# The four order tables of a recurrent stage, written anew

## The reference

```
h = layernorm(x) * (1 + ca) + sa;  x = x + ga * attn(h)
h = layernorm(x) * (1 + cb) + sb;  x = x + gb * moe(h)
# attn, per sequence and head (32 pairs), over 4 chunks of 64 tokens, one after the other:
gate = k @ w0;  hb = k @ w2;  hidden = silu(gate) * hb;  dhidden = v @ w1.T
G1 = (hidden * lr1).T @ v;  G0 = (k * lr0).T @ dgate;  G2 = (k * lr2).T @ dhb
wi = wi + newtonschulz(Gi, 2 steps)      # X = a X + (b A + c A A) X, with A = X X.T
wi = wi / norm(wi) * norm(wi at the start)
o  = (silu(q @ w0) * (q @ w2)) @ w1
# then: norm of o, projection, residual; routing logits; experts (64, top 6); combine
```

## Time and profile before

| | |
|---|---|
| median of 3 runs | 1771.67 us |
| the profiled execution | 1769.68 us, its span 1767.3 us |
| PE, DVE, ACT, POOL busy | 90%, 65%, 50%, 46% of the span |
| instructions | 40874 |
| recurrent stage | about 150 to 930 us of the span |

### The profile page before, as it was taken

How to read it: one execution, slowest core, us unless ns; L and a number is a source line. 1 busy time by engine, 2 the same in 40 slices (tenths; PEclk the granted TensorE clock), 3 DMA queues, 4 the chain that set the end, 5 groups by cost and what they waited for, 6 DMA issues and landing times. The chain is left out here.

```text
span 1767.3 us, 40874 instructions
## 1 busy us (share of the span) xinstructions
PE 1591.9 (90%) x11235; PEld 1184.7 (67%) x11235; DVE 1147.2 (65%) x4093; ACT 880.9 (50%) x2156; POOL 817.9 (46%) x882
## 2 busy tenths in 40 slices
PE   7995999888889888988862999999999999998997
PEld 4664667666666666666652677777777777776775
DVE  5664878788888788888864554444444444433887
ACT  4773767666666666666641333333333333332221
POOL 2322334566566566666675233333333343343333
PEclk9996999999999999999965999999999999999998
DMA  3864444444444532232224656556555656322996
GB/s 131 258 226 153 129 143 128 156 134 141 152 150 153 163 95 83 83 89 83 74 89 135 183 175 186 172 171 185 171 175 176 182 179 194 98 54 62 252 245 152
DMA packets 260031, 263.27 MB, mean 149 GB/s; under 512 B 83563, under 2 KB 231385, under 8 KB 259824
## 3 DMA queue, kind: packets, MB, share of 16 engines
q1 hardware_dynamic: 196016, 170.45, 33.4%
q0 software_dynamic: 21504, 51.18, 8.2%
q10 hardware_dynamic: 42304, 39.08, 8.1%
HBM read 141.78 MB, written 127.18 MB: 152 GB/s over the span
## 5 line engine op out<-in xcount | busy, mean ns | idle before, releaser
L1709 POOL DMA_INDIRECT scratch_y<-e_eo,e_goes x256 | 251.7, 983 | 405.3 <-ACT e_eo L1798 336.6
L1735 PE MATMUL e_psGU<-wgu,e_xT 128*128 x1024 | 352.1, 466 | 3.1 <-issue 2.3
L1846 DVE COPY e_hT<-e_psH 88x256 f32<-88x256 f32 x256 | 107.7, 421 | 338.6 <-PE e_psH L1744 242.2
L1751 PE MATMUL e_psD<-wd,e_hT 88*128 x1024 | 263.6, 379 | 0.0
L1735 PEld LDWEIGHTS e_psGU<-wgu,e_xT 128*128 128x128 f32 x1024 | 186.7, 190 | 87.6 <-issue 18.3
L1369 POOL TENSOR_TENSOR f_wnr<-f_wss,f_half 128x4 f32<-128x4 f32 x96 | 109.3, 1139 | 230.7 <-DVE f_wss L1192 230.1
L1359 POOL DMA_INDIRECT scratch_buf<-rows,dest x180 | 185.3, 1030 | 45.5 <-issue 43.7
L1787 ACT ACTIVATE e_sgm<-e_psGU 128x176 f32<-128x176 f32 x256 | 81.2, 317 | 238.5 <-PE e_psGU L1735 206.6
L1751 PEld LDWEIGHTS e_psD<-wd,e_hT 88*128 88x128 f32 x1024 | 173.8, 190 | 14.3 <-issue 0.3
L1798 ACT ACTIVATE e_eo<-e_psD 128x256 f32<-128x256 f32 x256 | 98.1, 383 | 161.8 <-issue 87.6
L1721 PEld LDWEIGHTS e_psX<-ident,e_xg 128*128 128x128 f32 x512 | 72.4, 142 | 76.7 <-issue 40.8
(11 more groups left out here) (303 smaller groups left out, 3773.2 us busy)
## 6 DMA issues: line engine op xcount, KB each, us to landing
e_xg<-scratch_buf ACTq DMA_DIRECT2D x256, 132.0 KB
scratch_y<-f_blank SPq DMA_DIRECT2D x64, 384.0 KB
c_g<-scratch_y SPq DMA_DIRECT2D x64, 384.0 KB, 6.1
...
```

The lines of the kernel that those rows point to most:

```text
L1709: pool.indirect_dma_start(out=T["y"], out_offset=bass.IndirectOffsetOnAxis(goes[:, n:n + 1], 0), in_=eo[:, n % OB, :], in_offset=None, bou ...
L1735: mm = pe.matmul(psGU[:, j % 2, 0:2 * F], xT[:, j % 2, k, :], wgu[:, bass.ds(buf, 1), k, :].rearrange("p b n -> p (b n)"), start=(k == 0), ...
L1751: mm = pe.matmul(psD[:, j % 2, 0:D], hT[0:FH, j % 2, k, :], wd[0:FH, buf, k, :].rearrange("p b n -> p (b n)"), start=(k == 0), stop=(k == 1))
L1846: v.tensor_copy(hT[0:FH, b, :, :].rearrange("p k t -> p (k t)"), psH[0:FH, b, 0:2 * P]).then_inc(htd, 1)
```

## The change

The four tables are replaced. The steps, their waits and the number of times each is issued stay as they are, but for a last "send" entry that issues nothing. The tables start at another point of the cycle (PE's now with the poly2's of lot 1 in the half headed by chain 1), and lags are raised by one where that needs it. Within the cycle entries change places, and the two halves, alike before but for the names of the chains, now differ. Cut to the parts of which the prediction speaks:

PE_ORDER, the half headed by chain 0 before (the other is its mirror), and both halves after:

```diff
-    ("x2t", 1, 1, 2), ("gram2", 1, 1, 1), ("x2", 1, 1, 2, 0), ("output", 1, 2, 1), ("poly2", 1, 1, 0),
-    ("gram2", 1, 1, 2), ("turn_o", 0, 2, 1), ("hidden_back", 0, 0), ("poly2", 1, 1, 1), ("poly2", 1, 1, 2),
-    ("last", 1, 1, 0), ("grads_0", 0, 0), ("project", 0, 2, 0), ("back", 0, 1, 2, 1), ("grads_1", 0, 0),
-    ("last", 1, 1, 1), ("grads_2", 0, 0), ("turn", 0, 0, 0, 1), ("grads_3", 0, 0), ("turn", 0, 0, 1, 0),
-    ("last", 1, 1, 2), ("gram", 0, 0, 0), ("turn", 0, 0, 2, 1), ("row_sums", 0, 0), ("gram", 0, 0, 1),
-    ("turn_x", 1, 3, 1), ("totals", 0, 0), ("read", 0, 1, 0), ("back", 1, 1, 0), ("gram", 0, 0, 2), ("back", 1, 1, 1),
-    ("gate", 1, 0), ("logits", 1, 3, 1), ("poly", 0, 0, 0), ("poly", 0, 0, 1), ("poly", 0, 0, 2), ("x2", 0, 0, 0, 1),
...
+    ("poly2", 0, 1, 1), ("poly2", 0, 1, 2), ("project", 1, 3, 0), ("back", 1, 2, 2, 1), ("grads_0", 1, 1),
+    ("grads_1", 1, 1), ("grads_2", 1, 1), ("last", 0, 1, 1), ("grads_3", 1, 1), ("turn", 1, 1, 0, 1),
+    ("row_sums", 1, 1), ("turn", 1, 1, 1, 0), ("gram", 1, 1, 0), ("last", 0, 1, 2), ("turn", 1, 1, 2, 1),
+    ("gram", 1, 1, 1), ("totals", 1, 1), ("back", 0, 1, 0), ("turn_x", 0, 3, 1), ("read", 1, 2, 0),
+    ("logits", 0, 3, 1), ("back", 0, 1, 1), ("gate", 0, 0), ("gram", 1, 1, 2), ("poly", 1, 1, 0), ("poly", 1, 1, 1),
+    ("poly", 1, 1, 2), ("x2", 1, 1, 0, 1), ("x2t", 1, 1, 0), ("x2t", 1, 1, 1), ("hidden_base", 0, 0),
+    ("x2", 1, 1, 1, 1), ("x2t", 1, 1, 2), ("gram2", 1, 1, 0), ("gram2", 1, 1, 1), ("x2", 1, 1, 2, 0),
+    ("output", 1, 2, 1), ("poly2", 1, 1, 0), ("gram2", 1, 1, 2), ("hidden_back", 0, 0), ("turn_o", 0, 2, 1),
+    ("poly2", 1, 1, 1), ("poly2", 1, 1, 2), ("last", 1, 1, 0), ("last", 1, 1, 1), ("grads_0", 0, 0),
+    ("grads_1", 0, 0), ("back", 0, 1, 2, 1), ("project", 0, 2, 0), ("grads_2", 0, 0), ("turn", 0, 0, 0, 1),
+    ("grads_3", 0, 0), ("turn", 0, 0, 1, 0), ("gram", 0, 0, 0), ("turn", 0, 0, 2, 1), ("row_sums", 0, 0),
+    ("last", 1, 1, 2), ("gram", 0, 0, 1), ("totals", 0, 0), ("turn_x", 1, 3, 1), ("back", 1, 1, 0), ("read", 0, 1, 0),
+    ("logits", 1, 3, 1), ("back", 1, 1, 1), ("gate", 1, 0), ("gram", 0, 0, 2), ("poly", 0, 0, 0), ("poly", 0, 0, 1),
+    ("poly", 0, 0, 2), ("x2", 0, 0, 0, 1), ("x2t", 0, 0, 0), ("x2t", 0, 0, 1), ("hidden_base", 1, 0),
+    ("x2", 0, 0, 1, 1), ("gram2", 0, 0, 0), ("x2t", 0, 0, 2), ("gram2", 0, 0, 1), ("x2", 0, 0, 2, 0),
+    ("output", 0, 1, 1), ("poly2", 0, 0, 0), ("turn_o", 1, 2, 1), ("hidden_back", 1, 0), ("gram2", 0, 0, 2),
+    ("last", 0, 0, 0),
```

ACT_ORDER:

```diff
-    ("xt", 1, 1, 2, 1), ("square", 0, 1, 2), ("h_keep", 0, 3, 1), ("read", 1, 2, 0), ("w", 0, 1, 0), ("w", 0, 1, 1),
-    ("l_keep", 0, 3, 1), ("gate", 0, 0), ("x2", 1, 1, 0, 1), ("o_scale", 0, 2), ("x2t", 1, 1, 0), ("x2t", 1, 1, 1),
-    ("x2", 1, 1, 1, 1), ("a2", 1, 1, 0), ("x2t", 1, 1, 2), ("a2", 1, 1, 1), ("output", 1, 2, 1), ("a2", 1, 1, 2),
-    ("o_square", 1, 2), ("b2", 1, 1, 0), ("o_keep", 0, 2, 1), ("b2", 1, 1, 1), ("x2", 1, 1, 2, 0), ("b2", 1, 1, 2),
-    ("square", 1, 1, 0), ("w", 0, 1, 2, 1), ("x", 0, 0, 0), ("x", 0, 0, 1), ("xt", 0, 0, 0, 1), ("x", 0, 0, 2),
...
+    ("xt", 1, 1, 2, 1), ("h_keep", 0, 3, 1), ("w", 0, 1, 0), ("w", 0, 1, 1), ("gate", 0, 0), ("l_keep", 0, 3, 1),
+    ("o_scale", 0, 2), ("read", 1, 2, 0), ("square", 0, 1, 2), ("x2", 1, 1, 0, 1), ("x2t", 1, 1, 0), ("x2t", 1, 1, 1),
+    ("x2", 1, 1, 1, 1), ("a2", 1, 1, 0), ("x2t", 1, 1, 2), ("output", 1, 2, 1), ("x2", 1, 1, 2, 0), ("a2", 1, 1, 1),
+    ("a2", 1, 1, 2), ("b2", 1, 1, 0), ("b2", 1, 1, 1), ("b2", 1, 1, 2), ("o_square", 1, 2), ("o_keep", 0, 2, 1),
+    ("square", 1, 1, 0), ("x", 0, 0, 0), ("w", 0, 1, 2, 1), ("square", 1, 1, 1), ("x", 0, 0, 1), ("xt", 0, 0, 0, 1),
...
+    ("read", 0, 1, 0), ("w", 1, 1, 1), ("l_keep", 1, 3, 1), ("o_scale", 1, 2), ("gate", 1, 0), ("x2", 0, 0, 0, 1),
+    ("x2t", 0, 0, 0), ("x2t", 0, 0, 1), ("x2", 0, 0, 1, 1), ("a2", 0, 0, 0), ("a2", 0, 0, 1), ("output", 0, 1, 1),
+    ("x2t", 0, 0, 2), ("b2", 0, 0, 0), ("o_keep", 1, 2, 1), ("a2", 0, 0, 2), ("x2", 0, 0, 2, 0), ("b2", 0, 0, 1),
+    ("o_square", 0, 1), ("square", 0, 0, 0), ("w", 1, 1, 2, 1), ("b2", 0, 0, 2), ("x", 1, 0, 0), ("x", 1, 0, 1),
+    ("x", 1, 0, 2), ("square", 0, 0, 1), ("xt", 1, 0, 0, 1), ("xt", 1, 0, 1, 0),
```

DVE_ORDER:

```diff
-    ("totals", 0, 0), ("update", 1, 1, 2), ("pick", 0, 3), ("factors", 1, 1, 1), ("renorm", 1, 1, 1),
-    ("norm_x", 0, 2), ("norms", 0, 0), ("a", 0, 0, 0), ("a", 0, 0, 1), ("a", 0, 0, 2), ("b", 0, 0, 0),
-    ("b", 0, 0, 1), ("row_norms", 1, 1, 2), ("b", 0, 0, 2), ("read", 0, 1, 0), ("place", 0, 3), ("factors", 1, 1, 2),
-    ("gate", 1, 0), ("slope", 1, 0), ("slope_2", 1, 0), ("both", 1, 0), ("token_dg", 1, 0), ("rows_x", 0, 2),
-    ("token_dhb", 1, 0), ("update", 0, 0, 0), ("token_hid", 1, 0), ("row_norms", 0, 0, 0),
...
+    ("token_hid", 0, 0), ("update", 1, 1, 1), ("row_norms", 1, 1, 0), ("squares", 0, 0, 0), ("gate_x", 0, 2, 0),
+    ("row_norms", 1, 1, 1), ("norm_x", 0, 2), ("squares", 0, 0, 1), ("squares", 0, 0, 2), ("factors", 1, 1, 0),
+    ("row_sums", 0, 0), ("renorm", 1, 1, 0), ("totals", 0, 0), ("update", 1, 1, 2), ("factors", 1, 1, 1),
+    ("pick", 0, 3), ("renorm", 1, 1, 1), ("norms", 0, 0), ("a", 0, 0, 0), ("a", 0, 0, 1), ("a", 0, 0, 2),
+    ("b", 0, 0, 0), ("b", 0, 0, 1), ("row_norms", 1, 1, 2), ("b", 0, 0, 2), ("read", 0, 1, 0), ("factors", 1, 1, 2),
+    ("place", 0, 3), ("gate", 1, 0), ("slope", 1, 0), ("token_hid", 1, 0), ("slope_2", 1, 0), ("rows_x", 0, 2),
+    ("both", 1, 0), ("update", 0, 0, 0), ("token_dg", 1, 0), ("token_dhb", 1, 0), ("gate_x", 1, 2, 0),
+    ("row_norms", 0, 0, 0), ("norm_x", 1, 2), ("squares", 1, 0, 0), ("update", 0, 0, 1), ("factors", 0, 0, 0),
```

POOL_ORDER:

```diff
-    ("row_root", 0, 1, 1), ("root", 1, 1), ("root_x", 1, 3), ("row_root", 0, 1, 2), ("send", 0, 0, 0),
-    ("renorm", 0, 1), ("send", 0, 0, 1), ("row_root", 1, 1, 0), ("root_o", 1, 2), ("send", 0, 0, 2),
-    ("row_root", 1, 1, 1), ("root", 0, 0), ("root_x", 0, 2), ("row_root", 1, 1, 2), ("send", 1, 0, 0),
-    ("renorm", 1, 1), ("send", 1, 0, 1), ("row_root", 0, 0, 0), ("root_o", 0, 1), ("send", 1, 0, 2),
...
+    ("root", 1, 1), ("send", 1, 1, 2), ("send", 0, 0, 0), ("root_x", 1, 3), ("row_root", 0, 1, 2), ("renorm", 0, 1),
+    ("send", 0, 0, 1), ("root_o", 1, 2), ("row_root", 1, 1, 0), ("row_root", 1, 1, 1), ("root", 0, 0),
+    ("root_x", 0, 2), ("send", 0, 0, 2), ("send", 1, 0, 0), ("row_root", 1, 1, 2), ("renorm", 1, 1),
+    ("send", 1, 0, 1), ("root_o", 0, 1), ("row_root", 0, 0, 0), ("row_root", 0, 0, 1),
```

More of the change, by code:

```diff
@@ L475 @@
-    ("gate", 1, 0), ("logits", 1, 3, 1), ("poly", 0, 0, 0), ("poly", 0, 0, 1), ("poly", 0, 0, 2), ("x2", 0, 0, 0, 1),
[3 rows of a table removed]
-    ("last", 0, 0, 0), ("grads_0", 1, 0), ("project", 1, 2, 0), ("back", 1, 1, 2, 1), ("grads_1", 1, 0),
-    ("last", 0, 0, 1), ("grads_2", 1, 0), ("turn", 1, 0, 0, 1), ("grads_3", 1, 0), ("turn", 1, 0, 1, 0),
-    ("last", 0, 0, 2), ("gram", 1, 0, 0), ("turn", 1, 0, 2, 1), ("row_sums", 1, 0), ("gram", 1, 0, 1),
-    ("turn_x", 0, 2, 1), ("totals", 1, 0), ("read", 1, 1, 0), ("back", 0, 0, 0), ("gram", 1, 0, 2), ("back", 0, 0, 1),
+    ("poly2", 0, 1, 1), ("poly2", 0, 1, 2), ("project", 1, 3, 0), ("back", 1, 2, 2, 1), ("grads_0", 1, 1),
@@ L502 @@
-    ("factors", 0, 1, 2), ("gate", 0, 0), ("slope", 0, 0), ("slope_2", 0, 0), ("both", 0, 0), ("token_dg", 0, 0),
-    ("rows_x", 1, 3), ("token_dhb", 0, 0), ("update", 1, 1, 0), ("token_hid", 0, 0), ("row_norms", 1, 1, 0), ("update", 1, 1, 1), ("squares", 0, 0, 0), ("gate_x", 0, 2, 0), ("squares", 0, 0, 1),
-    ("factors", 1, 1, 0), ("squares", 0, 0, 2), ("row_norms", 1, 1, 1), ("row_sums", 0, 0), ("renorm", 1, 1, 0),
-    ("totals", 0, 0), ("update", 1, 1, 2), ("pick", 0, 3), ("factors", 1, 1, 1), ("renorm", 1, 1, 1),
@@ L511 @@
-    ("squares", 1, 0, 2), ("row_norms", 0, 0, 1), ("row_sums", 1, 0), ("renorm", 0, 0, 0), ("totals", 1, 0),
-    ("update", 0, 0, 2), ("pick", 1, 3), ("factors", 0, 0, 1),
+    ("totals", 1, 1), ("pick", 1, 4), ("factors", 0, 1, 1), ("renorm", 0, 1, 1), ("norms", 1, 1), ("a", 1, 1, 0),
+    ("a", 1, 1, 1), ("a", 1, 1, 2), ("b", 1, 1, 0), ("b", 1, 1, 1), ("row_norms", 0, 1, 2), ("b", 1, 1, 2),
+    ("read", 1, 2, 0), ("gate", 0, 0), ("factors", 0, 1, 2), ("slope", 0, 0), ("slope_2", 0, 0), ("place", 1, 4),
@@ L513 @@
+    ("update", 0, 0, 2),
 )
 POOL_ORDER = (
[L516 to L519 removed]
+    ("root", 1, 1), ("send", 1, 1, 2), ("send", 0, 0, 0), ("root_x", 1, 3), ("row_root", 0, 1, 2), ("renorm", 0, 1),
```

7 lines of the change are left out of this document (2 added, 5 removed), and 10 rows, old and new, of tables (ACT_ORDER, PE_ORDER).

## The result

The changed kernel takes 1804.49 us (median of 4 runs, 1797.27 to 1812.39), the kernel before 1770.93 beside it (4 runs, 1767.56 to 1774.84): a ratio of 1.0185, 95% interval 1.0151 to 1.0219. Slower, where 1748 was forecast, with a range to 1786. The profiled execution has a span of 1794.9 us against 1767.3.

The account below looks back on a forecast made before the run. PE, busy for 90% of the span at full clock, bounds the kernel, so only its idle time can go; per half 1.76 us removed less 1.0 added is 0.76, 31 times 23.6 us: 1748 us, range 1722 to 1786.

Parts of the forecast that it names:

- Items 1 to 3: PE's waits before gram2, project and back go, as o_scale, x2 and logits move: 0.39, 0.74, 0.63 us a half.
- Rival B: Slower through ACT's o_keep: the spare bank is emptied late and PE stands before back; 1783 us, chance 0.20.
- Item 5: Adjacent POOL sends behind root hold PE's completions, so DVE waits for the first two polys: 0.45 us added a half.
- Item 8: Headed by 1, row_sums before the second turn makes PE wait for the third squares: 0.05 us added on the mean.
- Item 2: x2 of lot 2 evicted before b2 of lot 1 in both halves, removing the wait before project: 0.74 us a half.
- Items 6 and 7: New waits around gram2 of lot 2 (headed by 1) and last of lot 1 (headed by 0): 0.25 us added each.
- A: Rival: holds miss the new places, so the added waits are near zero; 54.6 us gained, 1717 us, chance 0.17.
- C: Rival: the new waits take back all; net 0 to 0.3 us a half, 1763 to 1772 us, chance 0.18.

Follow-up runs that it names:

- b_joined: The kernel before with grads_1 directly behind grads_0 in both halves: ratio 1.0322 where the kernel before takes 1771 to 1782 us, 1.0135 where it takes 1731 to 1732.
- a_again: The changed kernel, unchanged, on a chip where the kernel before takes 1731 to 1732 us; ratio 0.9993 to the kernel before.
- a_once_more: The changed kernel, unchanged, on another chip where the kernel before takes 1731 to 1732 us; ratio 1.0040 to the kernel before.
- a_rows_fill: The changed kernel with six products of a constant ahead of a row_sums wait in the half headed by 1; 1697.37 us, ratio 0.9812 to the kernel before.
- a_split: The changed kernel with grads_1 moved behind back and project in the half headed by 0; ratio 1.0408 to the kernel before.
- a_split2: The changed kernel with back and project between grads_0 and grads_1 in both halves; ratio 1.0092 to the kernel before.

## Why the prediction was wrong

**The steps that held.** Items 1 to 3 do what they say: the waits before gram2, project and back are 0.0, 0.0 and 0.6 us in some 22 halves. Rival B didn't come: back into the spare bank (L903 from spare) has 0.0 idle, so o_keep was never late. Ahead of the sends nothing holds, and the clock is low for as long in both kernels (20.7 us before, 20.4 after, from the first gate on). From there to the 8th row sums the changed kernel gains 6.0 us, near the 5.3 that 0.76 a half would give; the other 1.3 of the 7.2 lie ahead of the stage, which the change doesn't touch. Item 5 is sized right: behind the sends x2t waits 5.1 us, poly 3.2 and x2 1.2 in 22 halves, 0.43 a half, of 0.45. The order as such is better than I said on sort S: pairs without a fall 41.7 against 44.4, 1.35 a half in place of 0.76; on sort L 0.47 by the fit.

**The step that failed first is the one named as what would make it wrong: "if PE, DVE and ACT rows themselves last longer, which nothing here leads me to expect".** The PE rows do. The sum had no term for the clock. It took the 1.00 of the earlier trace rows as given, though the change put PE's idle time, which the kernel before has in pieces of up to 0.9 us and one of 1.8, into pieces of 1.2 and more, 20 of them in the stretch. Measured: 102.5 us at the lower clock, 0.40 for each, 41 us. Of the miss in the stretch (18.2 gained by forecast, 29.6 lost) that is by the fit 41 of 47.8. That standing is the cause is shown on sort S, at the row sums. On sort L, where most of the waiting is at the gradients, I have only that the falls stand right behind it and that b_joined brings 88.7 us at the lower clock by making that wait; no run filled or removed it there.

**The second: grads_1 behind grads_0 was not costed at all.** The prediction puts grads_0, grads_1 and grads_2 in a row in the half headed by 1, and grads_1 behind grads_0 in the other; each waits for a count that PE itself raises one step earlier, and item 5 had just found that what PE has finished is seen late while POOL sends. I applied that to DVE and ACT, and not to PE. Measured on sort L: 33.3 us in the groups, 1.5 a half; the join alone, in the kernel before, is worth +3.2% there and +1.35% on sort S.

**A premise: "a new order can give only the idle time of PE".** On sort S PE is busy for 40.6 us in each pair of the kernel before and for 39.3 in the first pair of a_again above, with the same products and the same clock. So about half of the 2.7 us that such a pair gained is busy time, in which products overlap more; their ends are modelled, so how much of it is real stays open.

**Mis-sized terms.** Item 8, row sums before the second turn: 0.05 forecast, 0.23 a half measured (0.53 against 0.31 before), and on sort S one wait of 1.48 in every pair. I took the three evictions "x" in a row as cover, but the row names DVE's squares (f_sq) as what PE waits for. It is the item that costs most on sort S, through the clock. Item 2: worth 0.74 on sort L, nothing on sort S. Items 6 and 7, 0.25 each, show no wait. Net, idle time fell by 1.7 us in the stretch where 18.2 was forecast. On sort S it fell from 45.9 (532.61 - 486.76, below) to 30.2 in a_again, by 15.7, near the forecast; both traces have 5232 records of PE there, while that of a_once_more has 5280 and shows 24.2.

```profile
308.08:840.69 532.61, 486.76 (x5232) 378.46 (x5281) 466.53 (x1393) 374.04 (x865) 351.45 (x361) 1.00 0.42 128
```

With few falls the order is worth what lies between the forecast and A, on sort S: a_rows_fill, the same order with the wait filled, is 1.9% below the kernel before, where 1748 is 1.3% and A's 1717 3.0% below 1770.93. C, the new waits take back all, is right for the idle time on sort L. None had the clock.

**What stays open.** Why the chips are of two sorts. Whether it is the send that holds PE's counts on the one: each held wait of over 1 us ends at most 1.4 us behind a send, but the sends stand at the same place of every half, DMA traffic runs beside them (0.78 of the DMA engines' time in the stretch at 498 us), and kernels without the sends weren't tried. What sets how long a fall lasts, and so why a_split has 253 us at the lower clock with waits no longer than the changed kernel's. Whether a_rows_fill, or a_split2 with its steps parted in both halves, beats the kernel before on sort L.
